# TensorE's loop over the key/value groups 1 to 6 of the second attention, written out while the other engines keep their loops

## What is computed

```python
x = x + attn(lora(x, A, B, adapter_ids), weight_qkv, weight_proj)          # attention over the batch axis
x = x + ffn(cond2(x, Wq, Wk, Wv, Wo, q_norm, k_norm, k_cache, v_cache, block_table, cache_seqlens), ...)
```

```python
k_all = concat([k_cache[block_table], k]); v_all = concat([v_cache[block_table], v])
probs = softmax(where(valid, q @ k_all.T * SCALE, -1e30))
out   = (probs @ v_all).reshape(B, S, HQ * D) @ Wo.T
```

## Time and profile before

| what | value |
|---|---|
| device time, median of 3 runs | 1665.09 us |
| lowest and highest | 1663.77 and 1668.67 us |
| span of the profiled execution | 1656.7 us |
| granted TensorE clock over the span | 0.982 |
| PE, PEld, DVE, ACT, POOL busy | 94%, 77%, 71%, 55%, 48% of the span |

### The profile page before, as it was taken

The page is one execution under the profiler, slowest core; times in us unless marked ns, Lnnn a source line. Parts: engine busy times, 40 slices in busy tenths (PEclk is TensorE's granted clock), DMA queues, the critical chain, the costliest instruction groups (busy, mean ns, idle before and its releaser), DMA issues.

```text
span 1656.7 us, 29874 instructions
## 1 busy us (share of the span) xinstructions
PE 1564.6 (94%) x8792; PEld 1270.6 (77%) x8792; DVE 1176.9 (71%) x2603; ACT 910.3 (55%) x2323; POOL 790.8 (48%) x1004
## 2 busy tenths in 40 slices
PE   6999899898999999999989999998999899989987
PEld 4777544446888788788878878887888788878875
DVE  1566762217888788788868878886888788878856
ACT  2555521115666566576656656665666566656631
POOL 0000003004666666666656656666666566656411
PEclk8999999998999999999999999999999999999999
DMA  7133122102222221222122212222221222131102
GB/s 259 65 127 139 39 85 81 57 7 67 69 70 65 62 72 56 67 77 72 51 80 69 70 60 74 68 62 62 75 75 48 80 73 65 49 90 49 52 6 84
DMA packets 69046, 119.23 MB, mean 72 GB/s; under 512 B 15339, under 2 KB 24939, under 8 KB 68851
## 3 DMA queue, kind: packets, MB, share of 16 engines
q1 hardware_dynamic: 52466, 83.37, 15.2%
q0 software_dynamic: 16384, 33.59, 7.0%
HBM read 109.56 MB, written 7.34 MB: 71 GB/s over the span
## 4 chain that ended last, share of the span: by engine, by line
PE 77%; DVE 7%; issue 6%; ACT 4%; POOL 4%; SPq 2%; DMA 0%; DVEq 0%; POOLq 0%; ACTq 0%
PE ps_t L857 12%; PE ps_o L657 9%; PE ps_o L659 8%; PE ps_o L658 8%; PE ps_o L814 4%; PE ps_q L814 4%; PE ps_q L659 3%; PE ps_q L658 3%; PE ps_q L657 3%; PE ps_a L657 2%; PE ps_a L658 2%; PE ps_a L659 2%; PE ps_a L695 2%; PE ps_b L657 2%; PE ps_b L659 2%
## 5 line engine op out<-in xcount | busy, mean ns | idle before, releaser
L1267 ACT ACTIVATE sm<-sm,mn 128x640 f32<-128x640 f32 x256 | 211.3, 826 | 264.5 <-DVE mn L1702 264.5
L568 POOL DMA_INDIRECT kraw<-in_L_cond_k_cache_dram,idx_a x200 | 197.3, 987 | 318.8 <-DMA mask_scratch<-maskall 233.5
L1595 DVE TENSOR_TENSOR pT_lo<-ps_t,pT_hi 128x512 fp32r<-128x512 f32 x320 | 219.7, 687 | 83.8 <-ACT pT_hi L1195 83.7
L568 POOL DMA_INDIRECT vraw<-in_L_cond_v_cache_dram,idx_a x200 | 197.7, 989 | 85.4 <-issue 46.3
L1195 ACT ACTIVATE pT_hi<-ps_t 128x512 fp32r<-128x512 f32 x320 | 188.6, 589 | 84.9 <-PE ps_t L857 84.8
L857 PE MATMUL ps_t<-ident,sm 128*128 128x128 f32 x1280 | 198.1, 277 | 8.1 <-ACT sm L1277 4.7
L857 PEld LDWEIGHTS ps_t<-ident,sm 128*128 128x128 f32 x1280 | 148.3, 141 | 56.0 <-DVE qT_lo L1595 16.3
L1702 DVE CUSTOM_DVE_ANT_0 sm<-ps_a,mask,qs 128x640 f32<-128x640 f32 x128 | 112.4, 878 | 39.9 <-PE ps_a L659 28.9
L657 PE MATMUL ps_o<-pT_lo,v_hi 128*128 128x512 f32 x320 | 130.6, 408 | 0.0
L659 PE MATMUL ps_o<-pT_hi,v_hi 128*128 128x512 f32 x320 | 126.2, 394 | 0.0
L658 PE MATMUL ps_o<-pT_hi,v_lo 128*128 128x512 f32 x320 | 125.6, 393 | 0.0
(11 more groups left out here) (235 smaller groups left out, 4184.3 us busy)
## 6 DMA issues: line engine op xcount, KB each, us to landing
tab<-tab_scratch SPq DMA_DIRECT2D x64, 256.0 KB, 2.7
wraw<-n_L_attn_weight_qkv_dram SPq DMA_DIRECT2D x8, 1536.0 KB, 7.1
wpraw<-_L_attn_weight_proj_dram SPq DMA_DIRECT2D x8, 1024.0 KB, 9.4
mask<-mask_scratch SPq DMA_DIRECT2D x64, 128.0 KB, 2.8
wtile<-in_L_cond_Wq_dram SPq DMA_DIRECT2D x28, 256.0 KB, 2.8
wtile<-in_L_cond_Wo_dram SPq DMA_DIRECT2D x28, 256.0 KB, 3.0
kraw<-in_L_cond_k_cache_dram,idx_a POOLq DMA_INDIRECT x200, 2.6
vraw<-in_L_cond_v_cache_dram,idx_a POOLq DMA_INDIRECT x200
```

What stands on the lines that cost most here:

```text
L568: pool.indirect_dma_start(raw[:, par, c, :], None, rows_d, bass.IndirectOffsetOnAxis(idx[:, k:k + 1].bitcast(U32), 0)).then_inc(arrived[pa ...
L1267: act.activation(sm[:, h, :], sm[:, h, :], ACT.Exp, bias=mn[:, h:h + 1], scale=-1.0, accum_out=den[:, h:h + 1]).then_inc(e_done, 1)
L1595: dve.tensor_tensor(lo, src, hi.bitcast(F32), ALU.subtract).then_inc(t_lo, 1)
```

## The change

On PE alone the loop over groups 1 to 6 becomes a Python loop, so the eight steps of the body stand in PE's program six times, with the group's number known in each. The matmuls and their order are the same; the branch and the register instructions that computed wait values and addresses from g are gone.

```diff
             for n in range(N):
                 step(0, n, True, False)
-            with pe.Fori(1, G - 1) as g:
+            for g in range(1, G - 1):
                 for n in range(N):
                     step(g, n, False, False)
             for n in range(N):
                 step(G - 1, n, False, True)
```

## The result

The changed kernel takes 1668.18 us (median of 20 runs, 1659.12 to 1674.47) against 1663.20 us (20 runs, 1658.54 to 1670.38): a ratio of 1.0027, 95% interval 1.0014 to 1.0039. By the interval it is slower by 2.3 to 6.5 us, where 6 us was forecast from a first median of 1665.09. A second timing of both kernels (experiment 10) gave 1.0019 (0.9998 to 1.0040), which by itself does not exclude that nothing changed.

What follows compares the result with a forecast made beforehand. PE, busy 94% of the span, was taken to bound the kernel, with POOL's return setting the seams. Five seams like seam 0 cost 5.1 us, up to 7.4 with POOL's idle time; about +6 on 1665.1 gave 1671 us, range 1661.5 to 1677.

Steps and rivals of the forecast that it cites:

- Idle time and clock of the PE branch, 26 us: Seams 1 to 5: PE's 3.5 us idle and 1.7 us slow clock each, 26 us if nothing else were late.
- Seam 0 as the pattern: Seams 1 to 5 become like seam 0, 43.5 us over two steps each: 5.1 us more than before in all.
- Sum, +6 us, from -0.7 us to the marker and +2.0 us behind it: Per seam, 0.7 us less to PE's own-key transpose (line 898), 2.0 us more in the step after; +6 us on the kernel.
- POOL's return, the unknown: POOL's extra idle time before its index list at five seams either goes (+5.1 us total) or stays (+7.4 us).
- Rival 1: Behind the gaps before line 898 PE's clock stays at the upper level: -2.6 to -6.4 us; chance 0.17.
- Rival 3: At seams where POOL returns late, longer gaps and slow stretches, 1.7 us more each: 1676 us; chance 0.15.
- Rival 2: PE does not wait for POOL, so the five seams give back most of the stall: about -19 us; chance 0.03.
- DVE and ACT at nothing: DVE and ACT keep their branches at the seams: no cost, or 0.3 us each without cover from PE's idle time.
- Register instructions and more code at nothing: Inside PE's steps, removing register instructions gains nothing and the body standing six times costs nothing.
- The upper bound of 12 us: Most that PE's longer code could cost: 0.5 us per two steps over 24 pairs, thought far off.

Runs made afterwards that it cites:

- experiment 10: The changed kernel timed again beside the kernel before: 1667.06 us against 1663.02 us, ratio 1.0019.
- kernel 2: POOL's loop alone written out, on the kernel before: 1655.30 us, 0.994 of the kernel before.
- kernel 3: POOL's loop written out too on the changed kernel, ACT and DVE still looped: 1637.05 us, 0.984 of the kernel before.
- kernel 1: PE, ACT, DVE and POOL loops all written out, SP alone looped, from the changed kernel: 1632.46 us, 0.981 of the kernel before.
- experiment 6: ACT and DVE written out too on the changed kernel, POOL still looped: 1667.21 us, 1.0026 of the kernel before.
- 5: On the kernel before, PE's loop body holds two groups and runs three times, so PE branches at seams 2 and 4 only: 1662.28 us in one execution.
- 4: On the changed kernel, 28 identity transposes fill PE's wait in the first step of groups 1 to 6: 1657.59 us, 0.996 of the kernel before.

## Why the prediction was right

*Idle time and clock of the PE branch, 26 us.* That much stands there, and the prediction was right that it is not what is won. With POOL written out it is worth 18 us, the step from kernel 2 to kernel 3.

*Seam 0 as the pattern.* Right. All five seams turned into it: scores at once, 1.2 to 1.6 us for the tile, then a wait of 3.0 to 3.8 us at line 898 (forecast 3 to 4.5) with the lower clock level behind each. Experiments 1, 2, 3 and 6 show that POOL sets it, 5 shows both kinds of seam in one execution, and 4 that the clock does the rest.

*Sum, +6 us, from -0.7 us to the marker and +2.0 us behind it.* The kernel before averages 23.9 and 18.6 us for the two steps over five seams. The trace after has 23.6 and 20.9, so -0.3 and +2.3 a seam, +10 us; the second trace of the same kernel (experiment 10) has 23.3 and 20.3, so -0.6 and +1.8, +6 us. The runs say +4.5 us by the ratio. The size was right within what one trace can tell; +2.0 lies between what the two traces show, -0.7 just beside it. That the time came so near 1671 us is in part luck: the 6 us are the middle between two ends and no mechanism of their own, and they were added to a first median that lay 1.9 us above that of the 20 runs.

*POOL's return, the unknown.* Its idle time is 29.9 us against 29.8 (29.1 in experiment 10), so it is POOL's own and stays, the upper of my two ends; that PE's refetch slowed it is not borne out. That end alone gives 7.4 us, a little over the runs.

*Rival 1 (the clock holds)* did not occur: each of the five gaps was followed by the lower level, in both traces. The shortest, 2.62 us, is that of seam 1 in experiment 10:

```profile
705.83 0.30 PE L898 MATMUL ps_b<-ident,rope_a 128*128 128x128 f32 x1 [2.62 <-DVE rope_a L1636]
```

```profile
707.00:711.00 4.00, 4.00 (x21) 3.96 (x20) 2.54 (x6) 0.86 (x2) 2.57 (x3) 0.59 0.08 27
```

*Rival 3 (longer gaps, and so longer slow stretches)* occurred in its second half only: seams 2, 3 and 5 had the longer stretch, and 21.1 to 21.3 us for the step behind, but no gap was longer than 3.75 us, and the length of the gap does not sort them (3.75 us at seam 1 had the short stretch, 3.02 at seam 5 the long one). In experiment 10 only seam 2 had it. That is a part of the scatter between the runs, and of why this trace lies above the median's share. *Rival 2* did not occur. The rule behind it (the Trainium skill, "Runtime: NRT & Kernel Launch", section "Instruction fetch mechanics", that kernels prefer full unrolling) holds here for the engines together and not for PE alone: with POOL and PE both written out the kernel gains 26 us, with PE alone it loses 4.

*DVE and ACT at nothing.* Right here, covered by the POOL wait (experiment 6); experiment 3 against 1 puts a price on it without that cover, about 1 us a seam where I had 0.3.

*Register instructions and more code at nothing.* The steps inside the groups stayed at 18.0 and 18.5 us; kernel 1, with four engines written out, shows the same. The upper bound of 12 us was empty, and my reason for it was wrong: the two pairs in the earlier trace rows are the same steps of their groups, with the same weight tiles. The pair of group 1, written out in the changed kernel, takes 36.5 us as it did looped, so the 0.5 us belong to group 0 (why is open).

## What to carry to other kernels

In this kernel a loop's branch back is paid by every compute engine that loops, at the same seam, side by side. Writing out the busiest one alone moved its wait to the next engine's return. So look at how late each engine comes back and at how long its way is to what the busiest one needs, and write out the one with the longest way too (here POOL, some 15 us; alone it gave 0.6%, with PE 1.6%). Where the trace holds one place that already looks like the change (here seam 0), measure that before adding up stalls. And an idle gap of TensorE can have a second price behind it (here 1.4 to 2.5 us of clock for gaps of 3.0 to 3.8 us), so where it can't be removed, filling it can be worth more than leaving it.

## What I had not expected

- Useless matmuls gain: 28 transposes in each of six gaps of 3 to 3.8 us took 1.4 to 2.5 us from the step behind it, 10 us in all.
- Moving 5 us of POOL's work off the path by reordering cost time, 0.3% against the changed kernel and 1.9% against the kernel before. POOL then stood waiting, 2.9 us at a seam and over 8 us in group 0, and PE felt it one step later.
- With both POOL and PE free of their branches, the stretch of two steps at seam 1 falls from 44.2 to 39.1 us. With ACT and DVE written out too it is 38.2 us, and that kernel (1632.46 us, 1.9% faster than before) is the best of this study.
